# Second cross attention: tokens quantised behind key 3, statistics ahead of the output's addition, output weights rounded in four portions

## The reference, cut to what matters

```python
ln_out = _ln(hidden_states, ln_w, ln_b)                       # layer norm of the tokens
def _fp8_linear_pertensor(x, wq, w_scale, in_scale):          # tokens quantised to fp8
    xq = _div_clamp_fp8(x, in_scale)
    return jnp.einsum('bsi,oi->bso', xq * in_scale, wq) * w_scale
qx = _ln(_fp8_linear_pertensor(ln_out, wqx, wqx_scale, qx_in_scale).reshape(b, s, g, hpg, d), qxln_w, qxln_b)
kvx = jnp.einsum('bsi,oi->bso', cond, w_kv_x)                 # cond: 257 context rows a batch
kx, vx = jnp.split(kvx, 2, axis=-1)
kx = _ln(kx.reshape(b, sc, g, d), kxln_w, kxln_b)             # g = 8 key groups, 16 heads, d = 128
xout = _gqa(qx, kx, vx).reshape(b, s, nh * d)                 # softmax(q k) v
cat = jnp.concatenate([core, xout], axis=-1)                  # core: self attention, computed before
catq = _div_clamp_fp8(cat, proj_smooth)
return jnp.einsum('bsi,oi->bso', catq, wproj) * (proj_in_scale * proj_w_scale)
```

## Time and profile before

| | us |
|---|---|
| median of three timed runs | 3549.98 (3548.26 to 3556.44) |
| the profiled execution's own time | 3552.97 |
| its span in the profile | 3551.2 |
| PE busy | 3275.0 (92%) |
| DVE busy | 2241.1 (63%) |
| ACT busy | 1868.7 (53%) |
| the second cross attention | about 1961 to 3203 |

### The profile page before, as it was taken

How to read it: one execution, slowest core, us unless ns; L and a number is a source line. 1 busy time by engine, 2 the same in 40 slices (tenths; PEclk the granted TensorE clock), 3 DMA queues, 4 the chain that set the end, 5 groups by cost and what they waited for, 6 DMA issues and landing times. The chain is left out here.

```text
span 3551.2 us, 74370 instructions
## 1 busy us (share of the span) xinstructions
PE 3275.0 (92%) x24736; PEld 2151.2 (61%) x24736; DVE 2241.1 (63%) x5883; ACT 1868.7 (53%) x5131; POOL 83.2 (2%) x134
## 2 busy tenths in 40 slices
PE   7999999999998998988888799999999999987799
PEld 4565666666653335556766466667666676656555
DVE  4556555555552226658887677777777777767832
ACT  4656656566553663336554555555555555534422
POOL 0000000000000000000000000000000000000000
PEclk8999999999998998999999899999999999998999
DMA  5333333334332002000000333333333333331000
GB/s 166 111 109 117 118 110 110 118 105 122 104 119 92 1 36 100 12 1 5 6 6 7 127 93 102 103 106 106 95 98 105 106 106 91 103 93 51 1 9 15
DMA packets 290410, 282.70 MB, mean 80 GB/s; under 512 B 20161, under 2 KB 235329, under 8 KB 288577
## 3 DMA queue, kind: packets, MB, share of 16 engines
q1 hardware_dynamic: 290240, 280.80, 26.0%
HBM read 206.02 MB, written 74.71 MB: 79 GB/s over the span
## 5 line engine op out<-in xcount | busy, mean ns | idle before, releaser
L480 PE MATMUL x_Kb<-x_cT,x_wk 128*128 128x257 f32 x3072 | 735.2, 386 | 41.0 <-ACT x_sq L732 20.6
L480 PEld LDWEIGHTS x_Kb<-x_cT,x_wk 128*128 128x128 f32 x3072 | 566.8, 190 | 237.9 <-issue 94.2
L508 PE MATMUL x_PC<-x_pT,x_cn 128*128 128x512 f32 x1024 | 475.9, 608 | 20.3 <-DMA x_pT<-x_probs_row 9.6
L746 ACT ACTIVATE x_pr<-x_pr,x_ntop 128x257 f32<-128x257 f32 x512 | 261.0, 510 | 369.7 <-DVE x_ntop L1018 190.0
L508 PEld LDWEIGHTS x_PC<-x_pT,x_cn 128*128 128x128 f32 x1024 | 185.5, 191 | 262.3 <-issue 251.4
L726 ACT ACTIVATE x_sq<-x_Kb 128x257 f32<-128x257 f32 x512 | 194.9, 381 | 164.5 <-DVE x_kT L994 157.7
L499 PE MATMUL x_Sb<-x_kT,x_qT 128*32 128x257 f32 (+1 forms) x4096 | 276.5, 384 | 4.9 <-DVE x_pr L1014 3.3
L994 DVE TENSOR_SCALAR x_kT<-x_Kb,x_vecs 128x257 f32<-128x257 f32 x512 | 240.1, 476 | 43.3 <-PE x_Kb L480 35.9
L752 ACT ACTIVATE x_pr<-x_pr,x_rps 128x257 f32<-128x257 f32 x512 | 241.1, 500 | 49.1 <-DVE x_rps L1024 45.2
L1034 DVE STREAM_TRANSPOSE x_turned<-x_pr 128x256 f32<-128x256 f32 x512 | 195.9, 420 | 60.5 <-ACT x_pr L752 42.9
L1048 DVE SCALAR_TENSOR_TENSOR x_pcT<-x_last,x_cT,x_PC 128x512 f32<-128x512 f32 x256 | 188.1, 737 | 43.6 <-PE x_PC L508 42.4
(11 more groups left out here) (316 smaller groups left out, 5790.5 us busy)
## 6 DMA issues: line engine op xcount, KB each, us to landing
x_probs_row<-x_turned SPq DMA_DIRECT2D x512, 128.0 KB, 2.3
x_pT<-x_probs_row SPq DMA_DIRECT2D x128, 512.0 KB, 3.8
x_cT<-in_ctxT SPq DMA_DIRECT2D x128, 257.0 KB, 4.3
x_cn<-in_ctx SPq DMA_DIRECT2D x128, 256.0 KB, 4.0
x_last<-x_last_row SPq DMA_DIRECT2D x128, 256.0 KB, 4.4
e_w<-in_e_w SPq DMA_DIRECT2D x3, 1152.0 KB, 7.7
c_staged_heads<-in_c_wqk SPq DMA_DIRECT2D x2, 1536.0 KB, 10.4
x_wq<-in_x_wq SPq DMA_DIRECT2D x1, 2048.0 KB, 8.0
```

Source lines behind the costliest of these rows:

```text
L480: m = pe.matmul(key_bank(j)[:, 0:SE], wk[:, c, g * HD:(g + 1) * HD], cT[:, b, c, :], start=c == 0, stop=c == HC - 1)
L508: m = pe.matmul(PC[h][:, :], cn[:, b % 2, c, h * P:(h + 1) * P], pT[:, c, :], start=c == 0, stop=c == KC - 1)
L746: act.activation(pr[:, v, :], pr[:, v, :], ACT.Exp, bias=ntop[:, u:u + 1], scale=1.0 if L1 else -1.0, accum_out=ps[:, u:u + 1]).then_inc(e ...
```

## The change

Three edits, all for the second cross attention alone. DVE's `token_stats(i + 2)` moves from the end of slot 2 to ahead of `add_output(i - 1)`. `quantise_tokens(i + 1)` in slot 0 moves from behind the copy of key 2 to behind that of key 3. ACT's `split_out` takes four heads at a time and is called at the end of each slot of tile 0, halves 0 and 1 in slots 0, 1 and 2, 3; GpSimd waits for two portions instead of one.

```diff
@@ scalar engine
-            def split_out(z):
-                act.wait_ge(out_weights, 16 * (z + 1))
-                act.activation(wo[0][:, 8 * z:8 * z + 8, :], wo_raw[:], ACT.Copy).then_inc(out_upper, 1)
+            def split_out(z, hs):
+                if hs[0] == 0:
+                    act.wait_ge(out_weights, 16 * (z + 1))
+                act.activation(wo[0][:, 8 * z + hs[0]:8 * z + hs[1], :], wo_raw[:, hs[0]:hs[1], :], ACT.Copy
+                               ).then_inc(out_upper, 1)
@@
                     norm_probs(i, s, 2)
-                if L1 and cur and not prev and s in (1, 3):
-                    split_out(s // 2)
+                if L1 and cur and not prev:
+                    split_out(s // 2, (s % 2 * 4, s % 2 * 4 + 4))
@@ gpsimd, split_out
-                pool.wait_ge(out_upper, z + 1)
+                pool.wait_ge(out_upper, 2 * (z + 1))
@@ vector engine, second_piece
+                if s == OUT_SLOT and L1 and nxt == 2:
+                    token_stats(i + 2)
                 if s == OUT_SLOT and prev:
                     add_output(i - 1)
@@ slot_to_output
-                    if g == 2 and s == 0 and nxt and L1:
+                    if g == 3 and s == 0 and nxt and L1:
                         quantise_tokens(i + 1)
@@ slot_from_output
-                if s == 2 and nxt == 2:
+                if s == 2 and nxt == 2 and not L1:
                     token_stats(i + 2)
```

## The result

| | before | changed |
|---|---|---|
| median of 8 timed runs each, us | 3553.44 | 3568.01 (3562.46 to 3578.43) |
| the profiled execution's own time, us | 3552.97 | 3568.18 |
| span, us | 3551.2 | 3566.4 |

The ratio is 1.004, with a 95% interval of 1.003 to 1.005: 14.6 us slower, 11 to 18. In the profile the second cross attention itself, from PE's first turn of tokens to the last addition, took 1255.2 us instead of 1236.8, +18.4. The two profiled executions as a whole differ by 15.2; the other 3 us lie in stages that the change doesn't touch, where two executions can differ by as much.

A forecast was written before the change was run, and what follows sets the result against it. PE was taken to bound the kernel, busy 939.65 of 964 us in the loop, its delays going into the time in full. Terms +20.6 + 10.2 - 8.0 + 2.7 = +25.5 us on 3549.98 gave 3575, range 3550 to 3590.

The forecast's parts named there:

- Part 1: Statistics ahead of DVE's addition push it behind the second hole, a late code packet: +26.7 us waiting, +20.6 net.
- What DVE's lead gives back: Within part 1: DVE leads PE into slot 3, so eleven key projection waits for ACT's squares go, -6.1 us.
- The clock: PE's new idle in the loop: six of twelve turns get a reduced-clock stretch, 1.7 us lost each, +10.2 us.
- Part 2: Slot 0, tokens quantised behind key 3's copy: PE's wait shrinks 0.53 us in each of fifteen tiles, -8.0 us.
- Part 3: Tile 0, output weights in four portions: ACT waits for the load, +2.7 us; +0.95 and -0.95 elsewhere; sum +2.7.
- (b): Rival on the loop's turns: the addition waits for the second packet but PE's clock holds, +15.3 us, 3565; chance 0.28.
- (a): Rival: holes are no code, or addition and statistics share a packet; the wait hides the statistics, -11.4, 3538.6; chance 0.1.

The follow-up runs named there:

- pad_b5: Kernel before plus five semaphore increments ahead of DVE's loop, no other edit: 3542.77 us, ratio 0.9967.
- e_quant: Kernel before with only the tokens quantised behind key 3: 3544.92 against 3553.09 us, ratio 0.9981.
- pad_a5: Changed kernel plus five semaphore increments ahead of DVE's loop: 3538.22 us against 3553.09 for the kernel before, ratio 0.9964.
- part 1 alone: Kernel before with only the statistics moved ahead of the output's addition: 3577.34 against 3553.09 us, ratio 1.0071.
- e_split: Kernel before with only the output weights rounded in four portions in tile 0: 3556.32 against 3553.09 us, ratio 1.0010.
- pad_b62: Kernel before plus sixty-two semaphore increments ahead of DVE's loop, single run: 3557.51 us beside 3555.34.
- pad_b50: Kernel before plus fifty semaphore increments ahead of DVE's loop, single run: 3543.13 us beside 3555.34.
- pad_q5: Kernel before plus five increments ahead of DVE's loop and tokens quantised behind key 3: 3534.86 against 3554.11 us, ratio 0.9942.
- pad_sq5: Changed kernel plus five increments ahead of DVE's loop, output weights in two portions as before: 3534.19 against 3554.11 us, ratio 0.9941.
- pad_b4: Kernel before plus four semaphore increments ahead of DVE's loop: 3572.78 against 3554.11 us, ratio 1.0048.

## Why the prediction was right, point by point

**Part 1.** Right in its mechanism and nearly in its size: 26.7 us of new waiting were foretold over twelve turns, 28.1 measured. The count of what fits into the first packet was off by one: the statistics' register step is merged with the loop's, so that L903 runs ahead of the hole and only the addition behind it. That put the start of the addition 0.2 us behind the end of the hole, where the sum had 0.26. The rest of the difference would be the length of the holes, which varies from turn to turn (the first one by 0.9 us in each of the two kernels).

**What DVE's lead gives back.** The waits of the key projections went, as foretold, but the term was too small. I took the 6.1 us that the trace shows; `pad_b5`, which only takes the holes away, shortens a turn by 0.74 to 0.8 us, 9 to 10 us over twelve. Laid side by side, one tile of `e_quant` and one of `pad_a5` differ at this place alone, by 1.21 us, where the trace of the first shows a wait of 0.93. Over ten turns (2216 to 2952) `e_quant` takes 7.6 us more than `pad_a5`, and its trace shows nine such waits with 4.7 us. So a wait of PE in the middle of a row of projections cost about 0.3 us more here than is shown as idle.

**The clock.** Six turns of twelve were taken, 10.2 us. The 1.7 us of each is a stretch of 3.40 us at 0.51; that six turns would have one no run shows: three did, one of them double, 6.8 us at most. The profile of part 1 alone had four between 2267 and 3033 us, 13.7 us at half clock together. The three waits ahead of the falls were 2.48, 2.79 and 2.80 us, but one of 2.76 us (to 2646.5) was followed by full clock, so the length of the wait doesn't tell them apart. Nor did two places of the kernel before, where a wait of 2.21 us (1.19 us of work in 3.40) was followed by 0.51 and idle of 2.25 us in two parts (1.75 us of work in 4.00) by full clock, so that the new idle seemed to lie between: the windows are of unequal length, and 3.40 us of the kernel before ahead of 2033.0 hold 1.15 us of work, less than the 1.19 of the row that was followed by half clock. The same idle at that place was followed by half clock in five of the twelve kernels. That the term came out near is partly luck.

**Part 2.** -8.0 foretold, -8.2 measured by the medians; 0.53 us a tile foretold, 0.52 to 0.54 a turn in the profiles (741.2 to 736.0 us over ten turns alone, 733.9 to 728.5 with the increments).

**Part 3.** +2.7 foretold; +3.2 (interval 0.4 to 6.8) measured alone, +1.3 to +2.8 in the profiles. The first portion cost 0.93 us as foretold and the shorter last one gave 0.85. The wait behind the load was over-sized: the load took 9.0 us in the changed kernel and 10.0 in `e_split`, not 10.1, and PE came to the place 2.4 us later in `e_split`, by what the first portion had cost and by the stretch at the lower clock ahead of it. The wait that was to be 2.7 us shrank to 1.07 in one profile and to nothing in the other. That stretch, 1.7 us of work, was in no term of the sum; it took the place of the wait, so that the +2.7 came out near by luck.

**The sum.** In the profile: 28.1 of waits, less 9.6 of key projections, 6.8 for the clock, less 8.0, 1.3 to 1.8 for part 3: about +19, against 18.4 measured for the stage. The terms come from several kernels and are known to about 1 us each, so that the sum closes this well is partly chance. Forecast +25.5; the two terms that were off, the clock and the key waits, explain 7 us. The measured medians give +14.6; what is left between that and the profile's 18.4 is mostly the 3 us of the other stages, which no part of the change explains. The forecast of 3575 was 7 us too high and inside the range, but the difference that it stands for was 11 us too large (+25.5 against +14.6): the three runs that it starts from have their median at 3549.98, the eight measured here at 3553.44, and those 3.5 us hid a part of the error.

**The rivals.** (b), the clock holds, 3565 or +15.3, came nearer to the measured 3568 and +14.6 than the forecast did. Its mechanism was not what happened: the clock fell in three turns, and the 7 us by which the forecast's sum is over the stage's are half the clock's and half the key waits'. (a) was wrong for the changed kernel, but its mechanism exists: where the holes are no longer there, the statistics cost nothing, as it says, and the time comes out as low as its 3538.6 or lower (3538.2 with part 3, 3534.2 without).

**The code that is kept.** A turn of 332 instructions ran without any packet with five and with fifty increments, and with five packets a turn with none, four and sixty-two. By the estimate of 128 instructions a packet, the first two turns touch three packets and the other three touch four, so that what is kept holds three packets. Whether it holds more, and what drops the head when a turn touches a fourth, isn't shown: that the head is dropped is inferred from this boundary and from the first hole, not seen. The packets that come and go with DVE's loop in this trace are 8 KB (46 in 0.38 MB). From the branch to the head it took 3.8 to 4.8 us in the kernel before and the changed one, 4.5 to 5.6 in `pad_b62`, and 0.3 where no packet came (`pad_a5`, `pad_b5`, `pad_b50`, `pad_q5`, `pad_sq5`).

## What to carry to other kernels

Where a sequencer's loop turns, look for register steps that wait for nothing and come late, and for packets of the instruction queue in each turn. Here five empty instructions ahead of the loop took away both holes and all five packets of a turn, and the addition for which PE waits cost 28.1 us of waiting in twelve turns, 2.3 us each, when it stood behind the second hole. Before you move work in such a loop, count the instructions from the head to the first hole behind it, and the packets that a turn touches. Here five instructions of nothing ahead of the loop were worth 11 us, more than either reordering inside it. Measure an edit of the order at two places of the code, or what you measure may be the place.

## What the runs showed of the hardware that I had not expected

- A loop of 332 instructions on VectorE ran without any instruction packet with fifty increments ahead of it, and with five packets a turn with sixty-two; by the estimate above it touches three packets of some 128 instructions in the first case and four in the second (`pad_b50` against `pad_b62`, 3543.1 against 3557.5 us, a single run each). In another pair of places 30 us of 3554 hang on one instruction (`pad_b4` against `pad_b5`, 3572.8 against 3542.8 us).
- The head's first instruction started 1.46 to 1.55 us behind the end of the turn's first instruction packet (kernel before, twelve turns), however late that packet came.
- ScalarE's loop (194 instructions a turn) shows no hole at its branch in any of the runs: 0.24 us at most from one instruction to the next there, in all twelve jumps.
- The second hole stood behind the fifth instruction from the head on and ended 2.3 to 2.6 us after the first had, in all twelve turns of the changed kernel and of the kernel before, whatever was executed in between.
- An idle of PE of up to 2.8 us in a busy stretch was followed by the lower clock (0.50) in three turns of twelve of the changed kernel, and by full clock in nine. The same two idles of 1.4 and 0.9 us in tile 0 were followed by the lower clock in five kernels and by full clock in seven.
